# Fused attention stage of a four-block transformer kernel: projections placed ahead of the attention's transposes, and the matrix's row added by GpSimd

## The reference

```python
# third block, linear attention; each batch's attention folds into one 256x256 matrix M_b and one row c_b
out = a @ M_b + c_b                       # a = layernorm(x)
x = x + layernorm(out)                    # layernorm(x): plain, no weights
# fourth block, attention half; its axes are (S, B, H) = (2, 2048, 256): the sequence axis is the one of length 2
ln1 = layernorm(h, ln1_w, ln1_b);  qkv = ln1 @ W_qkv     # 16 heads, 4 kv heads, 16 wide
attn = softmax(mask(q k^T / 4)) v
hidden = h + attn @ W_proj                # h = layernorm(x)
logits = layernorm(hidden, ln2_w, ln2_b) @ W_router
```

## Time and profile before

| | |
|---|---|
| median of 3 runs | 2599.53 us (2596.07 to 2607.96) |
| profiled execution, time | 2606.77 us |
| its span | 2604.7 us |
| PE / DVE / POOL / ACT busy over the span | 78% / 62% / 54% / 44% |
| mean granted TensorE clock | 0.841 of full |

### The profile page before, as it was taken

The page is one execution under the profiler, slowest core; times in us unless marked ns, Lnnn a source line. Parts: engine busy times, 40 slices in busy tenths (PEclk is TensorE's granted clock), DMA queues, the critical chain, the costliest instruction groups (busy, mean ns, idle before and its releaser), DMA issues. The chain is left out here.

```text
span 2604.7 us, 32123 instructions
## 1 busy us (share of the span) xinstructions
PE 2025.3 (78%) x8336; PEld 1347.7 (52%) x8337; DVE 1616.1 (62%) x3232; ACT 1143.3 (44%) x1965; POOL 1414.2 (54%) x1002
## 2 busy tenths in 40 slices
PE   6777869686869696874799999707798984799980
PEld 2445555555545464543466666405575663566650
DVE  1788887888888888885433223296833786422227
ACT  2686767676777767671111111123402441222222
POOL 1889898998999999981233333131301220344432
PEclk9887978796969697976899999858996886899995
DMA  2101111111111111114111111140000003112115
GB/s 71 36 31 46 34 50 33 45 33 46 33 47 35 43 37 36 42 37 186 52 44 44 44 46 45 62 160 12 5 19 4 17 25 153 46 64 64 62 51 193
DMA packets 77367, 139.09 MB, mean 53 GB/s; under 512 B 10449, under 2 KB 48465, under 8 KB 76450
## 3 DMA queue, kind: packets, MB, share of 16 engines
q1 hardware_dynamic: 63586, 100.19, 11.4%
q0 software_dynamic: 13632, 37.24, 4.5%
HBM read 105.38 MB, written 32.01 MB: 53 GB/s over the span
## 5 line engine op out<-in xcount | busy, mean ns | idle before, releaser
L778 DVE TENSOR_TENSOR_SCAN a_hs<-a_dA,a_carry,a_hs 128x512 f32<-128x512 f32 x512 | 637.3, 1269 | 28.1 <-POOL a_hs L400 23.7
L400 POOL TENSOR_TENSOR a_hs<-a_u,a_b_bc 128x1024 f32<-128x1024 f32 x258 | 624.2, 2421 | 0.4
L924 PE MATMUL a_h_ps<-k_ident,a_hs 128*128 128x128 f32 x2064 | 342.2, 319 | 183.0 <-DVE a_hs L778 114.1
L924 PEld LDWEIGHTS a_h_ps<-k_ident,a_hs 128*128 128x128 f32 x2064 | 285.6, 165 | 301.1 <-DVE a_hs L778 137.0
L554 ACT ACTIVATE a_dA<-a_delta,a_a_neg 128x512 f32<-128x512 f32 x512 | 351.6, 688 | 104.4 <-DVE a_hs L778 102.0
L412 POOL TENSOR_TENSOR a_acc<-a_acc,a_part 128x512 f32<-128x512 f32 x242 | 323.0, 1335 | 73.4 <-ACT a_part L568 72.3
L743 DVE SCALAR_TENSOR_TENSOR a_acc<-a_h_ps,a_c_tok,a_acc 128x512 f32<-128x512 f32 x242 | 177.4, 733 | 111.3 <-PE a_h_ps L924 111.1
L568 ACT ACTIVATE a_part<-a_h_ps,a_c_tok 128x512 f32<-128x512 f32 x242 | 165.6, 684 | 151.7 <-PE a_h_ps L924 136.0
L1224 POOL DMA_INDIRECT expert_rows<-m0e_ys,k_pair x71 | 70.1, 987 | 261.1 <-DVE m0e_ys L1276 249.3
L1243 ACT ACTIVATE m0e_gs<-m0e_g 128x512 f32<-128x512 f32 x71 | 42.4, 597 | 339.1 <-PE m0e_u L1316 253.9
L1286 DVE TENSOR_TENSOR m0e_h<-m0e_gs,m0e_u 128x512 f32<-128x512 f32 x70 | 48.1, 687 | 223.6 <-ACT m0e_gs L1243 223.6
(11 more groups left out here) (428 smaller groups left out, 3725.6 us busy)
## 6 DMA issues: line engine op xcount, KB each, us to landing
a_b_bc<-b_rows SPq DMA_DIRECT2D x132, 256.0 KB, 3.1
q_y<-expert_rows SPq DMA_DIRECT2D x32, 512.0 KB, 5.7
a_xl<-in_L_attn_x SPq DMA_DIRECT2D x9, 512.0 KB, 3.5
norm_rows<-a_shared SPq DMA_DIRECT2D x9, 512.0 KB, 2.9
m0w_up<-in_m_up SPq DMA_DIRECT2D x1, 4096.0 KB, 12.3
m0w_gate<-in_m_gate SPq DMA_DIRECT2D x1, 4096.0 KB, 22.2
m0w_down<-in_m_down SPq DMA_DIRECT2D x1, 4096.0 KB, 32.0
q_xl<-in_L_attn_x SPq DMA_DIRECT2D x8, 512.0 KB, 3.5
```

Of the source, the lines that this page charges most:

```text
L400: pool.tensor_tensor(hs[n % NBUF][:, half, :], u[s][:, half, :], b_bc[:, n % NBUF:n % NBUF + 1, :].broadcast_to([P, 2, T]), ALU.mult).then ...
L778: dve.tensor_tensor_scan(hs[k][:, c, :], dA[c][:], hs[k][:, c, :], carry[:, hf, c, n:n + 1], ALU.mult, ALU.add).then_inc(s_scan, 1)
L924: last = pe.transpose(hT_ps[j % 2][:, c * P:(c + 1) * P], hs[(n - 1) % NBUF][:, c, j * P:(j + 1) * P], ident[:])
```

## The change

One-row products (32 of them, two passes each) go from `apply`. Instead, before its first turn, TensorE makes both rows once on all 128 partitions (two products for each batch, into `o_ps`, which is free then), ScalarE copies them to SBUF (`row0`, `row1`), and in every step GpSimd adds the row to each batch's half of `r`, in place, after ScalarE's copy. The statistics of `r` on VectorE wait for these sums (`s_la`) instead of the copy (`s_lc`). On TensorE the projections of unit p move ahead of the "a" turn, and on ScalarE the copies of the projections move ahead of those of the "a" turn.

```diff
+        row = [m.sb(f"row{b}", [P, Q, D]) for b in range(B)]
...
             # GpSimd
+            pool.wait_ge(s_rowc, B)
             for n in range(N + LATE_R):
                 if has(n - 1):
...
                 if has(n):
                     s = n % 2
+                    for b in range(B):
+                        pool.wait_ge(s_lc, B * n + b + 1)
+                        pool.tensor_tensor(halves(r[s][:])[:, b, :], halves(r[s][:])[:, b, :], row[b][:].rearrange("p k d -> p (k d)"),
+                                           ALU.add).then_inc(s_la, 1)
                     pool.wait_ge(s_mv, n + 1)
...
             # ScalarE
+            act.wait_ge(s_row, 1)
+            for b in range(B):
+                act.activation(row[b][:], o_ps[b][:], ACT.Copy).then_inc(s_rowc, 1)
             copy_turned("l", 0, aT[0])
...
-                if has(o):
-                    if o >= 1:
-                        act.wait_ge(s_o[1], o)
-                    copy_turned("a", o, attT)
                 if has(p):
                     if p >= 2:
                         act.wait_ge(s_att, p - 1)
                     for q in range(Q):
                         act.wait_ge(s_q, Q * p + q + 1)
                         act.activation(qkv[p % 2][:, q, :], q_ps[q][:], ACT.Copy).then_inc(s_qc, 1)
+                if has(o):
+                    if o >= 1:
+                        act.wait_ge(s_o[1], o)
+                    copy_turned("a", o, attT)
...
             # VectorE
-                    dve.wait_ge(s_lc, B * (n + 1))
+                    dve.wait_ge(s_la, B * (n + 1))
...
             # TensorE
-                    pe.matmul(l_ps[:, k, :], ones[:], per.AR[:, b, :], start=True, stop=False)
                     for c in range(DC):
-                        last = pe.matmul(l_ps[:, k, :], aT[U % 2][:, c, t], per.AM[:, b, c, :], start=False, stop=c == DC - 1)
+                        last = pe.matmul(l_ps[:, k, :], aT[U % 2][:, c, t], per.AM[:, b, c, :], start=c == 0, stop=c == DC - 1)
...
+            for b in range(B):
+                for k in range(Q):
+                    last = pe.matmul(o_ps[b][:, k, :], ones[:], per.AR[:, b, :], start=True, stop=True)
+            last.then_inc(s_row, 1)
             turn("l", 0, a[0])
...
-                if has(o):
-                    pe.wait_ge(s_att, o + 1)
-                    pe.wait_ge(s_self, o + 1)
-                    turn("a", o, att[o % 2])
                 if has(p):
                     copied("p", p)
...
                         last.then_inc(s_q, 1)
+                if has(o):
+                    pe.wait_ge(s_att, o + 1)
+                    pe.wait_ge(s_self, o + 1)
+                    turn("a", o, att[o % 2])
...
-                        if o:
+                        if o == 0:
+                            pe.wait_ge(s_rowc, B)
+                        else:
                             pe.wait_ge(s_h, B * (o - 1) + b + 1)
```

More of the change, by code:

```diff
@@ L1966, in attend_phase @@
         s_tc = [m.sem(f"turned_copied{c}") for c in range(DC)]
+        s_row = m.sem("row_psum")
+        s_rowc = m.sem("row")
+        s_la = m.sem("applied_with_row")
         s_l = m.sem("applied_psum")
```

## The result

The changed kernel takes 2583.69 us (median of 7, 2582.25 to 2584.61) against 2596.56 for the kernel before beside it: 12.9 us less, ratio 0.9936 with the interval 0.9918 to 0.9953. The ratio is not that of the two medians: about a third of the executions of the kernel before are some 10 us longer than the rest, and its median does not show them. By the plain means of these runs the gain is 14.9 us, and the interval stands for 12 to 21. Forecast were 13 us less and, on the first median, 2586.5 us.

What follows compares the result with a forecast made beforehand. PE and DVE waited on each other through their order; POOL and DVE bound steps 5 to 7. 2.3 us ahead after step 7, 15.5 after step 10, less 2.5 for clock: 2599.5 - 13 = 2586.5 us, range 2578 to 2600.

Steps and rivals of the forecast that it cites:

- Price of a sum: Each 128x512 sum on POOL, both inputs in SBUF, takes 1.27 us, for all 16; 2.26 kept for the range.
- POOL's queue as the new wait: Before the statistics of `r`, DVE waits for POOL's powers then sums: 3.3 us in steps 6 and 7, 2.1 in step 5.
- Net of steps 5 to 7: Shift of the score products: later by 0.6 us in step 5, earlier by 1.9 in step 6, later by 2.2 in step 7.
- Steps 8 to 10: Projections run while DVE makes `att`, so waits before the scores go: gains of 5.2, 3.7 and 4.3 us.
- Step 10: Step 10 takes 13.0 us, bound by PE, against 17.3 before and 11.6 of DVE's work: gain 4.3 us.
- Start and steps 0 to 4: First turn late behind the row products, then shorter applies and less waiting: scores of step 4 come 3.2 us ahead.
- rival 3: Larger gain: clock rises early at the start and stays high in late steps, 20 us ahead, 2580 us; chance 15%.
- The clock term: In late steps, PE's gaps of about 1.2 us leave some work at half speed: 2.5 us off the gain.
- From profile to median: Profiled execution 2606.8 us lies 7.2 above the runs' median; the 13 us were taken from the median, 2599.5.
- Rival 1: Slower: POOL bounds everywhere, each sum 2.26 us, blocked or blocking, +15 us in steps 0 to 7, 2601.5 us; chance 8%.
- the rule on the shared access to SBUF: Two-input VectorE and SBUF-reading GpSimd instructions exclude each other; the new sums were held safe beside DVE's one-tensor-input normalisations.

Runs made afterwards that it cites:

- e2: Kernel before with only the order changed (projections and their copies ahead of the "a" turn), row products left on PE: 2586.2 us.
- e4: Changed kernel with POOL's two sums ahead of its two powers in each step instead of behind them: 2571.7 us.
- e5: Changed kernel without POOL's sums, DVE waiting for the copies again, the row missing from the result: 2566.2 us.
- the first trace: First profile of the kernel before, unchanged, from which the prediction was worked: execution of 2606.8 us, phase 236.2 us.
- e1: Kernel before, unchanged, run again for a second profile: execution of 2593.8 us, phase 226.1 us.
- e9: Kernel with sums ahead of the powers, router products of steps 7 to 9 moved behind the next step's "p" turn: 2571.4 us.
- e8: Kernel before with only the waits for the weights moved to their first use in step 3: 2596.6 us.
- e10: Kernel before with the row on GpSimd and sums ahead of the powers, old order of projections and "a" turn: 2593.9 us.
- e7: Kernel with sums first, its four row products behind the first turn and the weight waits moved to step 3: 2575.4 us.

## Why the prediction was right, and where it was not

The gain of 12.9 us met the forecast of 13, and the mechanism named for most of it was right: e2 shows that the order makes 10.5 of it. Two things were mis-sized and made up for each other: steps 0 to 4 brought more than forecast, and the trace that the sum was worked from had more to lose in steps 5 to 10 than a typical execution.

- *Price of a sum, 1.27 us.* Right: 16 of them, 1.26 to 1.32.
- *POOL's queue as the new wait, 3.3 us in steps 6 and 7.* Right: 3.06; e4 shows that it is the place behind the powers, not the sum. In step 5 the forecast was a wait of 2.1; the trace has none, but the four normalisations before it take 3.30 instead of 1.37, beside the two sums (2043.82 to 2046.37). Two of them took 1.36 and 1.38, each until a sum had ended; in e5, without sums, none of 64 took over 0.42. The sums blocked them: the same time on another row.
- *Net of steps 5 to 7: +0.6, -1.9, +2.2.* Against the first trace 0.35, -2.2, 1.9: right. Against e1 the lead shrinks by 3.3 us, since that trace had fewer waits to give up.
- *Steps 8 to 10: 5.2, 3.7, 4.3 ahead.* Against the first trace 5.3, 3.9, 4.0; against e1 4.1, 3.2, 3.7. The distances of 13 to 14 us are as forecast. Step 10 was put down to PE's chain (13.0): 13.3, with a wait of 1.17 for the projections, so PE did bind it. e9, on the kernel of e4, shows how close the other chain is: with PE's gap filled, step 10 goes from 12.3 to 11.5, the 11.6 that was forecast for DVE's work, and the phase gains only 0.3.
- *Start and steps 0 to 4: 3.2 ahead.* This term failed. It was 11.7 against the trace that it was made from, 7.1 against e1. The working kept the clock of step 0 low and had the statistics of `r` in step 0 at 0.3 behind; they came 5.5 ahead (15.2 us into the phase, 20.7 before). The clock rose 14 us earlier (8.4 us into the phase against 22.1), which was rival 3's mechanism, held there for 15 in 100. e8 shows the likely reason: a gap of 1.24 us that the working itself had filled, without asking what that does to the clock. The products also took 3.7 us, not 4.6.
- *The clock term, 2.5 off in the tail.* Step 8's projections were slow once (2.90 for four passes that take 1.46 at the high clock), step 9's too, step 10's not: right in kind, and covered in step 8, where DVE did not wait for them. Its size was not measured apart.
- *From profile to median.* The 13 us were taken off the median; the trace they came from was an execution 10 us above the median of these runs. The prediction saw that it lay high (7.2), and drew nothing from it. That 13 came out is partly luck: against e1, the forecast's 3 for the start, with the 3 lost in steps 5 to 7 and the 11 gained in steps 8 to 10, makes 11, and the early rise of the clock another 4.

Rival 1 was right that the sums and DVE block each other, and wrong in the size and the side: the sums took 1.26 to 1.32 in the kernel after and in e4 (once 1.42 in e10), and it was DVE that was held up, 1.3 us a step in e4. Of the rule on the shared access to SBUF: the trace agrees that two-input instructions collide. My reading of it, that a normalisation with one tensor input is safe, failed (1.38 us against 0.41 for the longest one). The page, SBUF — State Buffer of the Trainium skill, section "Who interferes with whom", does name such instructions among those that can collide, under conditions, which I had not drawn on; whether they hold here no run shows.

## What to carry to other kernels

When work moves to another engine, its price is first the place in that engine's queue: the same sums cost 12 us more behind two powers than ahead of them, and VectorE did not wait for the powers in either place. Taking work off one of two coupled chains pays only when the order lets the other follow: order and rows gave 10.5 and -1 alone, 12.9 together, 25 with the sums first. And one profile of a kernel whose executions spread, as these do over 17 us, is one draw: take a second before putting a number of 10 us on it.

## What the runs showed of the hardware that was not expected

A 128x512 sum on GpSimd holds up VectorE instructions that begin beside it, at most one of them per sum, until the sum has ended: a 128x256 normalisation took 1.38 instead of 0.41, a 128x256 product 1.20 instead of 0.39, a 128x64 one 0.68 instead of 0.21. The sums themselves stayed within 1.26 to 1.32, but for one of 1.42 in e10 and one of 1.36 in e7. A gap of 1.40 us between two groups of transposes went with 17 us more at 1.2 GHz behind it (e1 against e8). With the sums first the five executions lie within 1.2 us of each other (2570.7 to 2571.8); the 23 of the kernel before beside them spread over 13.
